# One fused two-layer kernel: the same instructions in other orders on all engines

## The chip, the cores and the metric

The kernel runs on one core of a Trainium2 chip. The metric is the device time of one execution in microseconds (us). Three runs of the kernel before took 1318.04, 1318.08 and 1318.75 us; the median is 1318.08.

## What is computed

Two layers over 64 sequences of 128 tokens with 256 features, each with a context of the same shape. Cut to what matters:

```python
# layer 0: attention with 16 heads of 16 features, over ctx
q, k, v = relu(x @ Wq + bq), relu(ctx @ Wk + bk), relu(ctx @ Wv + bv)
scores  = where(mask_of_query_row, q_ @ k_.T / 4, 1e-9)
x       = layernorm(softmax(scores) @ v_ + x) * gamma + beta
# layer 1, part 1: a Mamba-2 block
zxbcdt  = rms(x) @ in_proj_w                    # 256 -> 1288 features
z, xBC, dt = split(zxbcdt)
xBC     = silu(conv4(xBC))                      # causal, 4 taps, 768 features
h_t     = h_{t-1} * exp(dt*A) + (dt*xh_t) B_t ;  y_t = h_t C_t + D*xh_t   # 8 heads of 64
h       = x + rms(y * silu(z)) @ out_proj_w
# layer 1, part 2: attention with 8 heads of 32 features, over ctx
x       = h + softmax(ln(h) @ Wq @ (ctx @ Wk).T / sqrt(32)) @ (ctx @ Wv) @ Wo
```

## The kernel before

The 64 sequences are worked in 32 groups (g = 0 to 31) of two (b = 0, 1). Each engine has a program of its own: a list of small functions called in an order written out by hand, with waits on semaphores inside them. The body of `for g in range(NG - 9)` is the steady loop, 23 passes; the written-out lists before and behind it fill and empty the pipeline. In one pass an engine works on several groups at once: g+7 for the first projections, down to g+2 for the last part of the second attention.

TensorE's pieces (line of the matmul). Full array, 128 rows by 128 columns: `q`, `k`, `cp`, `z`, `k1` (six products each, twelve for z, L332: every weight and input is split in a high and a low part, three products for one), `v` (L375, L380), `v1` (L627), `o` (L573, and L575 for the sum of squares), `q1` (L587), `wp` (L692), `gm` (L531), `dp` (L490), and the transposes `tn` (L412), `ot`, `nt`, `bx`, `ht`, `tC` (L442) and `bd` (L501). Part of the array at a time: `sA` (L399) are the first attention's scores for the maxima, `sT` (L432, L436) the same scores transposed, `sC` (L648, L652) the second attention's scores. They use four groups of 32 rows. `av` (L456) and `oC` (L677) are the value products of the two attentions, on four groups of 32 columns, `y` (L556) the product of the Mamba block, on two groups of 64 columns. A matmul of plain float32 appears as two instructions in the trace, so one `av` is 8, one `sA` 16 and one `y` 16 instructions. `unread` repeats a product whose result nobody reads, in the lists before and behind the loop.

All results go to eight PSUM banks. The table `USES` fixes which piece uses which bank after which other one, and `bank(name, i, g)` gives the semaphore value at which the piece before in the same bank has been read. `sA(g, b)` takes four banks and waits for all four before its first matmul. For b = 0 one of them is bank 0, where `sT` number 7 of the group before stands; `eA(g, 7)` on ScalarE reads it (L1463). `y(g, b)` waits for `lg` on VectorE (L1024) and `xd` on GpSimd, `lg` for `gm` and `scan`; `yd` (L1044) reads y, and `v1` takes y's bank after it.

On the other engines: VectorE reads scores for maxima (`mA`, `mC`), does the convolution's taps (`tap`), the scan over time (`scan`), softplus (`dc`) and norms. ScalarE has exps (`eA`, `eC`), tanh (`th`, `zt`), copies out of PSUM and the high parts of the splits. GpSimd has the low parts (`lo_x`, `lo_c`, `lo_u`, `yl`), products by gates (`ga`, `xd`, `dx`) and powers. SyncE issues the transfers.

Of the kernel before, what the change touches and what calls it, by code (L numbers as in the profile page):

```python
# [12 lines left out]
NG = 32  # L13
# [24 lines left out]
def program(nc, a):  # L38
    with ExitStack() as ctx:
# [179 lines left out]
        def sync(e):  # L219
# [82 lines left out]
            load_x(1); load_c(1); load_t(0); load_m(1); load_x(2); load_m(2); load_c(2); load_c(3)  # L302
            load_m(3); load_x(3); load_t(1); load_x(4); load_m(4); dec_out(0); dec_in(0, 0); load_t(2); dec_in(0, 1)
            load_u(0); dec_out(1); load_c(4); dec_in(1, 0); dec_in(1, 1); load_u(1); load_t(3); load_x(5)
            dec_out(2); load_c(5); dec_in(2, 0); load_x(6); dec_in(2, 1); load_m(5); load_u(2); load_t(4)
# [10 lines left out]
            store(NG - 9); dec_out(NG - 6); load_c(NG - 3); dec_in(NG - 6, 0); load_m(NG - 3); load_m(NG - 2)  # L316
            dec_in(NG - 6, 1); load_x(NG - 2); load_u(NG - 6); load_t(NG - 4); load_c(NG - 2); store(NG - 8)
            dec_out(NG - 5); load_x(NG - 1); dec_in(NG - 5, 0); load_m(NG - 1); dec_in(NG - 5, 1); load_u(NG - 5)
            dec_out(NG - 4); load_c(NG - 1); load_t(NG - 3); dec_in(NG - 4, 0); dec_in(NG - 4, 1); load_u(NG - 4)
            load_u(NG - 3); load_t(NG - 2); store(NG - 7); dec_out(NG - 3); dec_in(NG - 3, 0); dec_in(NG - 3, 1)  # L320
            dec_out(NG - 2); store(NG - 6); load_t(NG - 1); load_u(NG - 2); dec_in(NG - 2, 0); dec_in(NG - 2, 1)
            store(NG - 5); dec_out(NG - 1); load_u(NG - 1); dec_in(NG - 1, 0); dec_in(NG - 1, 1); store(NG - 4)
# [4 lines left out]
        def tensor(e):  # L327
# [385 lines left out]
            k1(0, 1); bx(1, 0); av(2, 4); av(2, 5); av(2, 6); av(2, 7); sA(3, 0); ht(0, 0); ot(2, 1); q(4, 0)
            q(4, 1); ht(0, 1); k(4, 0); gm(1, 0); q1(0, 0); sA(3, 1); y(1, 0); v(4, 0); q1(0, 1); nt(2, 0); bx(1, 1)
            sC(0, 0); gm(1, 1); dp(2, 0); cp(2, 0); y(1, 1); cp(2, 1); o(1, 0); v1(0, 0); cp(2, 2); z(2, 0)
            tn(3, 0); cp(2, 3); o(1, 1); sT(3, 0); cp(2, 4); bd(2, 0); cp(2, 5); tn(3, 1); av(3, 0); av(3, 1)
            av(3, 2); av(3, 3); tC(0, 0); k(4, 1); ot(3, 0); z(2, 1); sT(3, 1); tC(0, 1); k1(1, 0); bx(2, 0)
            av(3, 4); av(3, 5); av(3, 6); av(3, 7); sA(4, 0); ot(3, 1); k1(1, 1); ht(1, 0); ht(1, 1); q(5, 0)
            tC(0, 2); q(5, 1); gm(2, 0); k(5, 0); sA(4, 1); y(2, 0); v(5, 0); q1(1, 0); q1(1, 1); gm(2, 1); bx(2, 1)
            nt(3, 0); tC(0, 3); sC(1, 0); oC(0, 0); oC(0, 1); dp(3, 0); cp(3, 0); cp(3, 1); y(2, 1); o(2, 0)  # L720
            v1(1, 0); z(3, 0); cp(3, 2); wp(0, 0); tn(4, 0); o(2, 1); cp(3, 3); sT(4, 0); bd(3, 0); cp(3, 4)
            cp(3, 5); tn(4, 1); av(4, 0); av(4, 1); av(4, 2); av(4, 3); tC(1, 0); k(5, 1); ot(4, 0); z(3, 1)
            sT(4, 1); tC(1, 1); k1(2, 0); bx(3, 0); av(4, 4); av(4, 5); av(4, 6); av(4, 7); sA(5, 0); k1(2, 1)
            ot(4, 1); ht(2, 0); ht(2, 1); q(6, 0); q(6, 1); tC(1, 2); k(6, 0); gm(3, 0); q1(2, 0); sA(5, 1); y(3, 0)
# [100 lines left out]
        def vector(e):  # L825
# [1291 lines left out]
```

## Time and profile before

| | |
|---|---|
| median of three runs | 1318.08 us |
| span of the profiled execution | 1319.5 us |
| TensorE matmuls busy | 1303.4 us (99%) |
| VectorE busy | 1193.6 us (90%) |
| ScalarE busy | 1131.2 us (86%) |
| GpSimd busy | 947.7 us (72%) |
| granted TensorE clock | 1.00 |

The span runs from the first to the last instruction. It is 1.4 us over the median of the runs. Busy is the time in which an engine had at least one instruction under way. Matmuls overlap: the next starts before the one before has left the array, so what a matmul costs is the time from its start to the start of the next, and not the duration beside it.

### The profile page before, as it was taken

The numbers are of one execution on the slowest core, as the hardware profiler recorded it, in microseconds if no ns is written. First come the engines' busy times: TensorE is split into PE (matmuls) and PEld (weight loads), VectorE is DVE, ScalarE is ACT, GpSimd is POOL, SyncE is SP. The second block draws the span as 40 slices with busy tenths as digits, with TensorE's granted clock in tenths as the row PEclk, the third lists the DMA queues.
The fourth block names the chain that finished last, engine by engine and source line by source line (L and its number), as shares of the span: only waits on it lengthen the run. The fifth ranks groups of instructions, "written<-read, shape, count | busy, mean of one in ns | idle before, by whom it ended". The sixth has DMA issues, their size and how long they took to land.

```text
span 1319.5 us, 43916 instructions
## 1 busy us (share of the span) xinstructions
PE 1303.4 (99%) x15877; PEld 1165.5 (88%) x15877; DVE 1193.6 (90%) x3032; ACT 1131.2 (86%) x3407; POOL 947.7 (72%) x1214
## 2 busy tenths in 40 slices
PE   8999999999999999999999999999999999999998
PEld 7888888999888898888998888899888889898887
DVE  6999999999999999999999999999999999999882
ACT  6778888898888898888898888899888899888866
POOL 4777777777777777777677777687777677677674
PEclk9999999999999999999999999999999999999999
DMA  6121122212122212122211122211122222011210
GB/s 208 48 74 50 50 74 78 78 49 67 50 70 78 78 50 66 50 70 78 78 57 59 50 70 78 78 60 57 50 70 78 77 82 62 17 51 58 66 49 25
DMA packets 41285, 87.03 MB, mean 66 GB/s; under 512 B 5744, under 2 KB 10992, under 8 KB 41072
## 3 DMA queue, kind: packets, MB, share of 16 engines
q1 hardware_dynamic: 40560, 83.93, 20.4%
q8 instruction: 129, 2.11, 0.7%
q14 instruction: 84, 0.69, 0.2%
q10 hardware_dynamic: 512, 0.31, 0.1%
HBM read 75.53 MB, written 8.68 MB: 64 GB/s over the span
## 4 chain that ended last, share of the span: by engine, by line
PE 92%; DVE 4%; POOL 2%; issue 1%; DMA 1%; ACT 1%; DVEq 0%; ACTq 0%; POOLq 0%
PE bank L332 28%; PE bank L442 11%; PE bank L573 7%; PE bank L432 5%; PE bank L399 5%; PE bank L456 5%; PE bank L556 5%; PE bank L587 4%; PE bank L692 4%; PE bank L627 3%; PE bank L380 3%; PE bank L648 3%; PE bank L677 2%; PE bank L490 2%; PE bank L436 1%; PE bank L531 1%
## 5 line engine op out<-in xcount | busy, mean ns | idle before, releaser
L991 DVE SCALAR_TENSOR_TENSOR ACC<-bank,cw,ACC 128x250 f32<-128x250 f32 (+2 forms) x576 | 264.5, 462 | 6.4 <-ACT ACC L1561 3.7
L332 PE MATMUL bank<-xnT,wnl 128*128 128x256 f32 x640 | 198.6, 310 | 1.7 <-DVE XC L1004 1.4
L1648 ACT ACTIVATE PC<-bank,stc 128x128 f32<-128x128 f32 x512 | 182.8, 388 | 8.0 <-DVE stc L1103 5.2
L332 PE MATMUL bank<-xnL,wnh 128*128 128x256 f32 x640 | 178.7, 279 | 0.0
L332 PE MATMUL bank<-xnT,wnh 128*128 128x256 f32 x640 | 178.3, 279 | 0.0
L835 DVE TENSOR_REDUCE sta<-bank 128x4 f32<-128x512 f32 x256 | 163.6, 672 | 2.8 <-PE bank L399 2.8
L1015 DVE TENSOR_TENSOR_SCAN L<-DB,id 128x1024 f32<-128x1024 f32 x64 | 146.6, 2290 | 2.2 <-DMA DB<-dec_scratch 2.2
L1967 POOL TENSOR_TENSOR PC<-PC,stc 128x512 f32<-128x512 f32 x128 | 132.4, 1043 | 11.7 <-DVE stc L1110 11.5
L1463 ACT ACTIVATE PTA<-bank 128x512 f32<-128x512 f32 x256 | 133.5, 629 | 6.8 <-PE bank L436 3.9
L332 PEld LDWEIGHTS bank<-xnT,wnl 128*128 128x128 f32 x640 | 120.4, 188 | 21.4 <-issue 16.2
L1922 POOL TENSOR_TENSOR XH<-XH,dtt 128x512 f32<-128x512 f32 x64 | 81.0, 1265 | 56.6 <-ACT XH L1578 56.6
L332 PEld LDWEIGHTS bank<-xnL,wnh 128*128 128x128 f32 x640 | 120.8, 189 | 0.1
L332 PEld LDWEIGHTS bank<-xnT,wnh 128*128 128x128 f32 x640 | 120.1, 188 | 0.0
L1648 ACT ACTIVATION_READ_ACCUMULATOR PC<-bank,stc 128x1 f32 x512 | 116.7, 228 | 0.0
L1847 POOL TENSOR_TENSOR cL<-cT,cH 128x512 fp32r<-128x512 f32 x31 | 59.0, 1903 | 76.8 <-ACT cH L1395 76.8
L1561 ACT ACTIVATE ACC<-bank,cw 128x256 f32<-128x256 f32 x192 | 110.6, 577 | 2.2 <-PE bank L332 1.5
L1931 POOL TENSOR_TENSOR Y<-Y,SZ 128x512 f32<-128x512 f32 x64 | 85.9, 1342 | 18.8 <-DVE Y L1044 16.1
L1937 POOL TENSOR_TENSOR Yl<-Y,Yh 128x512 fp32r<-128x512 f32 x64 | 82.2, 1285 | 17.4 <-ACT Yh L1606 17.4
L1449 ACT ACTIVATE NT<-bank,sel 128x128 fp32r<-128x128 f32 x256 | 73.6, 382 | 21.5 <-PE bank L412 21.5
L1662 ACT ACTIVATE PTC<-bank 128x512 f32<-128x512 f32 x128 | 78.8, 622 | 15.3 <-PE bank L442 15.2
L1103 DVE TENSOR_REDUCE stc<-bank 128x4 f32<-128x512 f32 x128 | 84.3, 681 | 6.9 <-PE bank L652 6.7
L1569 ACT ACTIVATE bank<-ACC 128x256 f32<-128x256 f32 x192 | 79.6, 418 | 11.1 <-DVE ACC L991 10.8
(210 smaller groups left out, 4757.7 us busy)
## 6 DMA issues: line engine op xcount, KB each, us to landing
DB<-dec_scratch SPq DMA_DIRECT2D x64, 512.0 KB, 4.0
cT<-in_cT SPq DMA_DIRECT2D x64, 256.0 KB, 2.7
xt<-in_xt SPq DMA_DIRECT2D x32, 256.0 KB, 3.7
out_x<-X SPq DMA_DIRECT2D x32, 256.0 KB, 4.0
xT<-in_xT SPq DMA_DIRECT2D x31, 256.0 KB, 4.1
QM<-qm_rows SPq DMA_DIRECT2D x31, 128.0 KB, 4.0
XC<-in_win SPq DMA_DIRECT2D x2, 644.0 KB, 6.8
PTC<-in_wout SPq DMA_DIRECT2D x2, 256.0 KB, 4.6
```

Source lines behind the costliest of these rows:

```text
L332: mm = e.matmul(t[:, c0:c0 + T], wt[:, k, m:m + 128], x[:, k, :], start=(n == 0), stop=(n == 5))
L442: mm = e.transpose(t[:, c0 + i * 128:c0 + (i + 1) * 128], src(i), ident[:, :])
L573: e.matmul(t[:, 0:256], x[:, kk * 128:(kk + 1) * 128], w[:, kk, :], start=(n == 0), stop=(n == 11))
L835: e.tensor_reduce(sta[ns % 4][:, 4 * j:4 * j + 4], t[:, :].rearrange("p (i k) -> p i k", i=4), AX_X, ALU.max, negate=True).then_inc(s_mA, 1)
L991: e.scalar_tensor_tensor(out=w, in0=t[:, 0:T].rearrange("p (b t) -> p b t", b=NB)[:, :, 0:125 + k], scalar=cw[:, c, k:k + 1], in1=w, op0=A ...
L1015: e.tensor_tensor_scan(L[:, :, :].rearrange("p h t -> p (h t)"), DB[b][:, :], id8[:, :, :].rearrange("p h t -> p (h t)"), 0.0, ALU.mult, A ...
L1103: e.tensor_reduce(stc[g % 4][:, 4 * i:4 * i + 4], t[:, :].rearrange("p (i k) -> p i k", i=4), AX_X, ALU.max, negate=True).then_inc(s_mC, 1)
L1463: e.activation(PTA[n % 4][:, :, :], t[:, :].rearrange("p (i k) -> p i k", i=4), ACT.Exp).then_inc(s_eA, 1)
L1561: e.activation(ACC[n % 3][:, :, :], t[:, 0:T].rearrange("p (b t) -> p b t", b=NB), ACT.Identity, bias=cw[:, c, 4:5], scale=cw[:, c, 3:4]). ...
L1648: op = e.activation(PC[n % 4][:, p, :], t[:, p * 128:(p + 1) * 128], ACT.Exp, bias=stc[g % 4][:, 4 * i + p:4 * i + p + 1], accum_out=stc[g ...
L1931: e.tensor_tensor(cv(Y[:, :]), cv(Y[:, :]), SZ[:, :, b * 128:(b + 1) * 128], ALU.mult).then_inc(s_ga, 1)
L1967: e.tensor_tensor(PC[n % 4][:, :, :], PC[n % 4][:, :, :], stc[g % 4][:, 16 + 4 * i:20 + 4 * i].unsqueeze(2).to_broadcast([128, 4, 128]), A ...
```

## The change

No function changes. The calls stand in another order in all five programs, in the loop and in the lists before and behind it; their number and kind are the same. TensorE's loop, cut to the part that differs (the first and last calls of the body are as before):

```diff
                 bx(g + 4, 0)
                 av(g + 5, 4)
                 av(g + 5, 5)
+                sA(g + 6, 0)
                 av(g + 5, 6)
                 av(g + 5, 7)
-                sA(g + 6, 0)
                 ht(g + 3, 0)
                 k1(g + 3, 1)
                 ot(g + 5, 1)
                 q(g + 7, 0)
                 ht(g + 3, 1)
                 q(g + 7, 1)
+                tC(g + 2, 2)
                 k(g + 7, 0)
-                tC(g + 2, 2)
                 gm(g + 4, 0)
                 q1(g + 3, 0)
                 sA(g + 6, 1)
+                v(g + 7, 0)
                 y(g + 4, 0)
-                v(g + 7, 0)
+                q1(g + 3, 1)
                 bx(g + 4, 1)
-                q1(g + 3, 1)
+                nt(g + 5, 0)
                 tC(g + 2, 3)
-                nt(g + 5, 0)
+                oC(g + 2, 0)
+                sC(g + 3, 0)
+                oC(g + 2, 1)
                 gm(g + 4, 1)
-                sC(g + 3, 0)
-                oC(g + 2, 0)
-                oC(g + 2, 1)
                 cp(g + 5, 0)
                 dp(g + 5, 0)
                 y(g + 4, 1)
                 cp(g + 5, 1)
                 o(g + 4, 0)
+                v1(g + 3, 0)
                 z(g + 5, 0)
-                v1(g + 3, 0)
+                wp(g + 2, 0)
                 cp(g + 5, 2)
-                wp(g + 2, 0)
                 tn(g + 6, 0)
```

Of the other engines' loops, the moves that the text below speaks of:

```diff
 # VectorE
+                mA(g + 7, 4)
                 x2(g + 6, 1)
-                mA(g + 7, 4)
-                yd(g + 5, 0)
                 mA(g + 7, 5)
                 mA(g + 7, 6)
                 mA(g + 7, 7)
+                yd(g + 5, 0)
                 scan(g + 5, 1)
...
                 mC(g + 4, 1)
-                mC(g + 4, 2)
                 d0(g + 6, 0)
                 d0(g + 6, 1)
+                nm(g + 7, 1)
+                mC(g + 4, 2)
                 rC(g + 4, 0)
                 tap(g + 6, 0)
-                nm(g + 7, 1)
 # ScalarE
                 hx(g + 2, 0)
+                split_c(g + 6)
                 pC(g + 1, 1)
-                split_c(g + 6)
...
+                v1e(g + 2, 0)
+                zt(g + 4, 0)
                 th(g + 4, 1)
-                zt(g + 4, 0)
-                v1e(g + 2, 0)
 # GpSimd
-                nC(g + 2, 1)
                 lo_u(g + 3)
                 qm(g + 6, 0)
                 r2(g + 3, 1)
+                lo_x(g + 7)
+                hr(g + 3, 0)
                 qm(g + 6, 1)
-                hr(g + 3, 0)
-                lo_x(g + 7)
+                nC(g + 2, 1)
                 hr(g + 3, 1)
 # SyncE
                 load_c(g + 6)
+                store(g)
+                load_m(g + 6)
                 dec_out(g + 3)
                 dec_in(g + 3, 0)
-                load_m(g + 6)
                 load_x(g + 7)
+                load_t(g + 5)
                 load_u(g + 3)
                 dec_in(g + 3, 1)
-                load_t(g + 5)
-                store(g)
```

The lists before and behind the loop are rearranged in the same manner, the places of `unread` and of the warming matmuls among them.

## Rows read from the trace of the kernel before

**Rows 1.** The page's busy times: us (share of the span) xinstructions.
```profile
PE 1303.4 (99%) x15877; PEld 1165.5 (88%) x15877; DVE 1193.6 (90%) x3032; ACT 1131.2 (86%) x3407; POOL 947.7 (72%) x1214
```

**Rows 2.** Busy time of the engines in three stretches: ahead of the loop, loop, behind.
```profile
0.00:206.00 206.00, 199.31 (x2384) 177.46 (x2385) 182.60 (x457) 166.37 (x467) 144.79 (x195) 1.00 0.26 82
206.00:1114.00 908.00, 907.92 (x11220) 814.27 (x11218) 845.45 (x2161) 803.25 (x2438) 665.22 (x851) 1.00 0.21 66
1114.00:1319.00 205.00, 196.21 (x2284) 173.72 (x2275) 165.58 (x415) 161.60 (x505) 137.68 (x170) 1.00 0.16 50
```

**Rows 3.** Waits, whole span: total us, times, longest.
```profile
PEld bank L456 <- ACT PTA L1463: 6.6, 33, 0.3
```

**Rows 4.** Timeline of TensorE, one pass: start us, us; av x4, sA, ht.
```profile
606.68 1.21 PE L456 MATMUL bank<-PTA,V 128*32 128x128 f32 x32
607.82 1.15 PE L399 MATMUL bank<-KT,QT 32*128 32x256 f32 x16
608.90 0.44 PE L442 MATMUL bank<-ident,xh 128*128 128x128 f32 x2
```

**Rows 5.** The same pass: q1, sA, y, v.
```profile
613.33 1.03 PE L587 MATMUL bank<-HT,wq 128*128 128x256 f32 x4
614.29 1.15 PE L399 MATMUL bank<-KT,QT 32*128 32x256 f32 x16
615.36 1.09 PE L556 MATMUL bank<-L,XH 128*64 128x128 f32 x16
616.39 0.50 PE L375 MATMUL bank<-vbias,onesr 128*128 128x512 f32 x1
```

**Rows 6.** The same pass: q1, tC, gm, sC, oC x2, cp, y.
```profile
618.53 1.03 PE L587 MATMUL bank<-HT,wq 128*128 128x256 f32 x4
619.40 0.60 PE L442 MATMUL bank<-ident,PC 128*128 128x128 f32 x4
...
620.27 0.39 PE L531 MATMUL bank<-XC 128*128 128x128 f32 x2
620.59 1.17 PE L648 MATMUL bank<-K1T,Q1T 32*128 32x128 f32 x32
...
621.91 1.08 PE L677 MATMUL bank<-PTC,V 128*32 128x128 f32 x32
622.92 0.38 PE L332 MATMUL bank<-xnT,wnl 128*128 128x256 f32 x1
623.14 0.28 PE L332 MATMUL bank<-xnL,wnh 128*128 128x256 f32 x1
623.26 0.28 PE L332 MATMUL bank<-xnT,wnh 128*128 128x256 f32 x1
...
624.61 1.09 PE L556 MATMUL bank<-L,XH 128*64 128x128 f32 x16
```

**Rows 7.** The other av run: whole, its second half, its last, tn.
```profile
638.87 1.08 PE L456 MATMUL bank<-PTA,V 128*32 128x128 f32 x32
...
639.33 0.62 PE L456 MATMUL bank<-PTA,V 128*32 128x128 f32 x16
...
639.55 0.40 PE L456 MATMUL bank<-PTA,V 128*32 128x128 f32 x8
...
639.88 0.33 PE L412 MATMUL bank<-ident,NM 128*128 128x128 f32 x1
```

**Rows 8.** Weight loads of the first av run's end [idle before <-releaser].
```profile
607.46 0.16 PEld L456 LDWEIGHTS bank<-PTA,V 128*32 128x32 f32 x8 [0.19 <-ACT PTA L1463]
```

**Rows 9.** Timeline of ScalarE: the four exps for this run.
```profile
605.28 2.13 ACT L1463 ACTIVATE PTA<-bank 128x512 f32<-128x512 f32 x4
```

**Rows 10.** Timeline of VectorE: lg(1) and yd(1).
```profile
622.70 1.21 DVE L1024 TENSOR_TENSOR L<-L,bank 128x1024 f32<-128x1024 f32 x1
...
626.41 0.69 DVE L1044 TENSOR_TENSOR Y<-bank,DX 128x512 f32<-128x512 f32 x1
```

**Rows 11.** Line 399: duration ns min/median/max, first and last start.
```profile
L399 PE MATMUL bank<-KT,QT x1024: 374/374/479, 14.2 to 1206.3; 32*128 32x256 f32 x171
```

More of the change, by code:

```diff
@@ L319, in sync @@
[L319 to L322, printed above, removed]
+            dec_out(NG - 6); load_c(NG - 3); dec_in(NG - 6, 0); store(NG - 9); load_u(NG - 6); load_x(NG - 2)
@@ new lines, in sync @@
+            dec_in(NG - 6, 1); load_m(NG - 3); store(NG - 8); load_x(NG - 1); dec_out(NG - 5); load_c(NG - 2)
+            load_t(NG - 4); load_m(NG - 2); dec_in(NG - 5, 0); load_t(NG - 3); load_u(NG - 5); dec_in(NG - 5, 1)
+            load_m(NG - 1); dec_out(NG - 4); load_c(NG - 1); dec_in(NG - 4, 0); store(NG - 7); load_u(NG - 4)
+            dec_in(NG - 4, 1); dec_out(NG - 3); load_t(NG - 2); dec_in(NG - 3, 0); store(NG - 6); load_t(NG - 1)
+            dec_in(NG - 3, 1); load_u(NG - 3); dec_out(NG - 2); dec_in(NG - 2, 0); load_u(NG - 2); dec_in(NG - 2, 1)
@@ L323, in sync @@
+            dec_out(NG - 1); store(NG - 5); dec_in(NG - 1, 0); dec_in(NG - 1, 1); store(NG - 4); load_u(NG - 1)
             store(NG - 3); store(NG - 2); store(NG - 1)
@@ new lines, in scalar @@
+            de(0, 1); de(0, 2); ac(0, 1); nt_(1, 0); dq(0, 0); th(0, 0); ac(0, 2); th(0, 1); qe(2, 1); zt(0, 0)
+            dd(0, 0); ac(0, 3); da(0, 0); ac(0, 4); th(0, 2); eA(1, 0); eA(1, 1); eA(1, 2); eA(1, 3); th(0, 3)
+            ac(0, 5); oa(1, 0); th(0, 4); nt_(1, 1); split_c(3); th(0, 5); ke(2, 1); zt(0, 1); eA(1, 4); eA(1, 5)
+            eA(1, 6); eA(1, 7); xhe(0, 0); oa(1, 1); n1(1, 0); qe(3, 0); qe(3, 1); n1(1, 1); nx(1, 0); xhe(0, 1)
+            nx(1, 1); ve(3, 0); nh(1, 0); nh(1, 1); qq(0, 0); yh(0, 0); de(1, 0); de(1, 1); de(1, 2); ac(1, 0)
@@ new lines, in scalar @@
+            ke(3, 0); dq(1, 0); ac(1, 1); th(1, 0); yh(0, 1); qq(0, 1); th(1, 1); zt(1, 0); ac(1, 2); nt_(2, 0)
+            split_x(4); dd(1, 0); ac(1, 3); th(1, 2); split_u(0); da(1, 0); eA(2, 0); eA(2, 1); ac(1, 4); eA(2, 2)
+            eA(2, 3); th(1, 3); ac(1, 5); oa(2, 0); nt_(2, 1); split_c(4); th(1, 4); th(1, 5); zt(1, 1); ke(3, 1)
+            eA(2, 4); eA(2, 5); eA(2, 6); eA(2, 7); hx(0, 0); hx(0, 1); n1(2, 0); oa(2, 1); xhe(1, 0); he(0, 0)
+            qe(4, 0); qe(4, 1); he(0, 1); ke(4, 0); q1e(0, 0); n1(2, 1); xhe(1, 1); nx(2, 0); ve(4, 0); nx(2, 1)
@@ new lines, in scalar @@
+            q1e(0, 1); nh(2, 0); nh(2, 1); yh(1, 0); split_x(5); qq(1, 0); eC(0, 0); ac(2, 0); de(2, 0); de(2, 1)
+            de(2, 2); eC(0, 1); dq(2, 0); ac(2, 1); eC(0, 2); th(2, 0); yh(1, 1); qq(1, 1); th(2, 1); split_u(1)
+            zt(2, 0); v1e(0, 0); dd(2, 0); ac(2, 2); nt_(3, 0); eC(0, 3); da(2, 0); th(2, 2); ac(2, 3); eA(3, 0)
+            eA(3, 1); eA(3, 2); eA(3, 3); ac(2, 4); th(2, 3); oa(3, 0); ke(4, 1); ac(2, 5); pC(0, 0); nt_(3, 1)
+            th(2, 4); th(2, 5); hx(1, 0); zt(2, 1); eA(3, 4); eA(3, 5); eA(3, 6); eA(3, 7); split_c(5); he(1, 0)
@@ new lines, in scalar @@
+            oa(3, 1); pC(0, 1); xhe(2, 0); hx(1, 1); qe(5, 0); qe(5, 1); he(1, 1); pC(0, 2); q1e(1, 0); n1(3, 0)
+            n1(3, 1); ke(5, 0); nx(3, 0); ve(5, 0); nx(3, 1); q1e(1, 1); pC(0, 3); nh(3, 0); nh(3, 1); xhe(2, 1)
+            qq(2, 0); yh(2, 0); eC(1, 0); oT(0, 0); ac(3, 0); ac(3, 1); de(3, 0); de(3, 1); eC(1, 1); de(3, 2)
+            eC(1, 2); qq(2, 1); dq(3, 0); zt(3, 0); th(3, 0); yh(2, 1); ac(3, 2); th(3, 1); v1e(1, 0); split_u(2)
+            eC(1, 3); dd(3, 0); nt_(4, 0); ac(3, 3); da(3, 0); th(3, 2); eA(4, 0); eA(4, 1); eA(4, 2); eA(4, 3)
@@ new lines, in scalar @@
+            split_c(NG - 3); xhe(NG - 6, 0); oa(NG - 5, 1); hx(NG - 7, 1); n1(NG - 5, 0); he(NG - 7, 0); qe(NG - 3, 0)
+            qe(NG - 3, 1); he(NG - 7, 1); pC(NG - 8, 2); q1e(NG - 7, 0); nx(NG - 5, 0); ke(NG - 3, 0); n1(NG - 5, 1)
+            nx(NG - 5, 1); ve(NG - 3, 0); xhe(NG - 6, 1); q1e(NG - 7, 1); nh(NG - 5, 0); pC(NG - 8, 3); nh(NG - 5, 1)
+            yh(NG - 6, 0); qq(NG - 6, 0); oT(NG - 8, 0); eC(NG - 7, 0); split_x(NG - 2); ac(NG - 5, 0); de(NG - 5, 0)
+            eC(NG - 7, 1); de(NG - 5, 1); ac(NG - 5, 1); de(NG - 5, 2); eC(NG - 7, 2); yh(NG - 6, 1); v1e(NG - 7, 0)
@@ new lines, in scalar @@
+            split_u(NG - 5); v1e(NG - 6, 0); zt(NG - 4, 0); split_x(NG - 1); dd(NG - 4, 0); ac(NG - 4, 2)
+            nt_(NG - 3, 0); eC(NG - 6, 3); da(NG - 4, 0); ac(NG - 4, 3); th(NG - 4, 2); eA(NG - 3, 0); eA(NG - 3, 1)
+            eA(NG - 3, 2); eA(NG - 3, 3); ac(NG - 4, 4); ac(NG - 4, 5); th(NG - 4, 3); oa(NG - 3, 0); nt_(NG - 3, 1)
+            pC(NG - 6, 0); th(NG - 4, 4); ke(NG - 2, 1); zt(NG - 4, 1); split_c(NG - 1); th(NG - 4, 5); eA(NG - 3, 4)
+            eA(NG - 3, 5); eA(NG - 3, 6); eA(NG - 3, 7); hx(NG - 5, 0); pC(NG - 6, 1); xhe(NG - 4, 0); oa(NG - 3, 1)
@@ L1829, in gpsimd @@
+            eC(NG - 1, 3); pC(NG - 1, 0); v1e(NG - 1, 0); pC(NG - 1, 1); pC(NG - 1, 2); pC(NG - 1, 3); oT(NG - 1, 0)
         def gpsimd(e):
```

626 lines of the change are left out of this document (292 added, 334 removed).

## The prediction

> **What bounds the kernel now.** I read the busy times of the page first: TensorE is busy for 1303.4 of 1319.5 us [rows 1]. The table of stretches then says where the rest is [rows 2]: 6.7 us idle in the first 206 us, 8.8 in the last 205, and 0.1 in the 908 us between, which are the 23 passes of the steady loop (39.5 us each). The granted clock is 1.00 in all three, the upper level of 2.4 GHz. In the loop VectorE has 845 and ScalarE 803 us of work for TensorE's 908. So one pass lasts as long as TensorE's matmuls take one after the other, and a change of order matters by what it does to the time from one matmul's start to the next. The waits that TensorE does pay in the loop are small: the one with the longest total at the weight loads of the value products is 6.6 us in 33 places [rows 3]; a run of four av that has it takes 1.14 us (606.68 to 607.82) where one without takes 1.01 [rows 4, 7].
>
> **How a piece's time depends on its neighbour.** I read starts in TensorE's timeline and subtract. Two kinds of pieces exist. Full-array ones (q, k, v, cp, z, all transposes, gm, q1) use 128 rows and columns. Part-array ones use four groups of 32 rows (sA, sT, sC), four of 32 columns (av, oC) or two of 64 columns (y).
>
> - A full-array piece pays when a part-array one follows. Four q1 matmuls take 0.87 us before a transpose (618.53 to 619.40) and 0.96 before sA (613.33 to 614.29) [rows 5, 6]. Price of that edge: 0.09.
> - A full-array piece pays when it follows a part-array one: the first product after oC holds the array 0.22 us (622.92 to 623.14), the next one 0.12 (to 623.26) [rows 6]. Price 0.10.
> - A part-array run pays at both of its ends whatever stands there. Four av between full-array pieces: the first two 0.46, the third 0.22, the last 0.33, together 1.01 [rows 7]. So the last costs 0.11 over the middle one and the first 0.02. Two oC take 1.01 as well, though they stand behind sC and not behind a full-array piece [rows 6]. sA takes 1.07 before y and 1.08 before a transpose, and the sA behind av is no shorter than the one behind q1 [rows 4, 5]. y takes 1.03 behind sA and in front of v [rows 5].
>
> The last point is what this change turns on: a part-array piece beside an unlike part-array piece pays as much as beside a full-array one. The Trainium skill says the same, in TensorEngine Tiling (Array Packing), Key Properties: "Changing tiling mode (not just tile) drains the TensorE". By that sentence the count of changes of shape is the thing to sum, and the trace agrees, at 0.13 to 0.2 us for a pair of edges.
>
> **The change part by part.** Nothing is added or removed. In TensorE's loop I count the places where the array's shape changes: 17 in a pass before, 20 after.
>
> 1. sA(g+6,0) goes between the second and third of four av. One run of av becomes two: a second last (+0.11) and a second first (+0.02). sA itself stays at 1.08. +0.13.
> 2. sC goes between the two oC, with the same sum for oC: +0.13. gm moves behind the last oC and takes over the entry that cp paid; tC takes over the exit that gm paid. Nothing for those.
> 3. v goes between sA(g+6,1) and y, which stood together, and q1 follows y. v's entry behind sA is the one it had behind y. New are v's exit (0.09) and the entry of q1 (0.10, that of the product behind oC; q1's are twice as long, so bounds 0 and 0.2): +0.19.
> 4. Full-array pieces changed among themselves (tC before k, nt before tC, v1 before z, wp before cp): no change of shape, so 0 for each. A first product behind another kind of full-array piece could cost up to the 0.10 of an edge; bounds -0.1 and +0.1 a pass.
>
> Sum 0.45 us a pass, 0.15 per change of shape. Over 23 passes 10.4. The written-out orders before and behind the loop have 31 changes of shape more than before (157 before, 188 after, counted from the diff): at 0.15 each 4.7. Together 15.1 us.
>
> 5. A wait moves. sA(g+6,0) takes four banks at once, one of them the bank of sT piece 7, which the eighth exp, eA(g+5,7), frees. In the pass shown the four exps end at 605.28 + 2.13 = 607.41 and the load for the waiting av follows at 607.46 [rows 8, 9]. After the change sA is next in line at 607.25 (the av run starts at 606.68 [rows 4], and two av take 0.24 + 0.33). It would start at about 607.46, 0.21 late, and behind it wait av 6 and 7. The 0.13 that av 7 loses there today goes, because it is then 1.3 us later. Net +0.08, which I round to 0.1 a pass, 2.8 us for the 28 groups that have this order or nearly this. Bounds: 0, if ScalarE reaches its exps earlier, and 0.3.
>
> 6. VectorE: mostly small exchanges; its instructions keep their durations, and it is not the bound in the loop [rows 2]. One chain gets tight. y(g+4,1) needs lg(1) (1.21 us), which needs gm(g+4,1). Today lg starts at 622.70 and ends at 623.91, and y starts at 624.61: 0.70 to spare [rows 6, 10]. After, gm is just ahead of cp and dp, so from its start to y there are 0.22 + 1.69 = 1.91 us, out of which 0.49 go for gm, some 0.1 for the signal and 1.21 for lg: 0.1 to spare. I take 0, bounds 0 and 0.3 a pass. The yd behind it (626.41) then comes some 0.7 later, and v1, which needs its bank and is itself earlier, has 0.3 left by the same subtraction.
>
> 7. ScalarE, GpSimd and the queue of transfers: split_c before pC, v1e before zt, nC(1) behind hr, store ahead of load_m. Each piece moved has over 0.5 us until TensorE needs it; two are nearer, xhe(1) before oC(0) and xhe(0) before q, at 0 to 0.1. At nothing, with bounds of 0 and 0.1 a pass each. Stores wait for fin of a much earlier group and hold back only loads for groups two to three passes ahead.
>
> Sum: 15.1 + 2.8 = 17.9 us on the profiled 1319.5, which is 1337.4. The profile's span is 1.4 over the median of the three runs (1318.08), so the time should be **1336 us**.
>
> **Rivals.**
>
> *New waits add up* (items 6 and 7). In favour: the chain gm, lg, y has 0.1 left of 0.7, and a late lg pushes yd, ga and o. Against: each is under 0.1 by my sums, and each pass is now longer, which gives every other engine 0.6 us more. At 0.3 a pass over 28 passes 8.4: 1345 us.
>
> *The ends gain.* TensorE idles 15.5 us outside the loop [rows 2], and every engine's order there is new. If half of it goes, 7.8 us: 1329 us. For: the pool is there. Against: most of those waits are of filling and emptying the pipeline, which no order shortens.
>
> *Unlike pieces hide each other*, the other side. If a piece sandwiched between unlike part-array pieces (sA between av, sC between oC) had neither edge to pay, because its groups load while the others still run, then four edges would go: 0.11 out of the column-shaped piece, 0.10 into the row-shaped one (sA's matmuls last 374 ns at the median and 479 at most, which I take for the first of a run [rows 11]), 0.11 out of it taken like av's, 0.02 into the next; 0.34 a sandwich, 0.68 a pass. With the 0.45 that come, -0.23 a pass, -6.4 over 28: 1312 us. It decides from 0.45 saved a pass on. The Trainium skill has a rule this way: TensorE: Matmul & The Clock Gate, Part 3, has weight loads overlap running matmuls when the row groups differ. The same edges stand in the trace at full price, so this needs the new neighbours to behave as the old ones don't.
>
> *The order hardly matters*: TensorE's loop stays at 39.5 because the extra edges fall into time lost anyway. Against: there is 0.1 us of idle in 908. 1318 us.
>
> **How the numbers follow.** Forecast 1336 with 0.57 (own range 1331 to 1340), new waits 0.22, the ends 0.12, hiding 0.05, no matter 0.04. 0.2% is 2.6 us, about what a measurement of this kernel can tell from none. Slower 0.91, same 0.04, faster 0.05. The range reaches from the case of the ends less the error of the 31 edges there (1327) to the waits with a little on top (1348).
>
> **What would show it.** Right: passes of 40.0 to 40.2 us instead of 39.5; each run of two av at 0.57 and each oC at 0.57; v before y over 0.09 longer than today; a wait of sA on the exps of about 0.2 in most passes. Wrong: sA between av shorter than 1.07; a pass below 39.8; a wait in front of y or v1 of over 0.1; idle outside the loop that changes by more than 5 us.

## The result and the profile after

The changed kernel takes 1394.82 us (median of 4 runs, 1393.70 to 1398.23) against 1318.17 for the kernel before on the same chip: ratio 1.058, 95% interval 1.0564 to 1.0596. It is slower, as forecast, but by 76.6 us and not by 18, and 47 us outside the range.

The page's busy times, to hold against [rows 1]:

```profile
PE 1332.0 (96%) x15877; PEld 1167.2 (84%) x15877; DVE 1269.7 (91%) x3032; ACT 1130.8 (81%) x3407; POOL 1023.3 (74%) x1214
```

The three stretches, cut where the loop starts and ends now (the loop's first k has moved from 205.8 to 225.0 us, the first piece behind the loop from 1114.7 to 1177.1):

```profile
0.00:225.00 225.00, 206.22 (x2383) 178.74 (x2384) 191.94 (x460) 166.98 (x467) 148.83 (x195) 0.99 0.23 78
225.00:1177.00 952.00, 926.69 (x11226) 815.60 (x11225) 903.87 (x2159) 803.17 (x2439) 728.53 (x850) 1.00 0.19 62
1177.00:1391.00 214.00, 199.09 (x2273) 172.86 (x2271) 173.94 (x415) 160.69 (x503) 145.94 (x170) 1.00 0.15 50
```

What the reader is to see: the same instructions, and in the loop the clock as before [rows 2] (ahead of it 0.99 for 1.00: one stretch of 3.4 us at the lower level of 1.2 GHz, from 17.3 us on), but TensorE has 25 us idle in the loop where it had 0.1, and VectorE and GpSimd are *busy* for 58 and 63 us longer in it without an instruction more. Of TensorE's 18.8 us of extra busy time in the loop 10.8 are the changes of shape, counted below; the rest isn't broken down. The idle 25 are new. A pass lasts 41.4 us (952.1 / 23) where it lasted 39.5. So the loop is 43.2 us longer, the lists ahead of it 19.2 and those behind it 9.9.

The waits of the whole span (total us, times, longest), to hold against [rows 3]:

```profile
PEld bank L573 <- issue: 19.5, 27, 1.0
PEld bank L399 <- DVE K1T L1092: 15.9, 23, 0.8
```

Before, L573 waited 0.8 us in 4 places and L399 never for K1T. L573 is `o`, the output projection; L399 is `sA`, which now waits for a bank that VectorE's kk1 (K1T) frees. By TensorE's starts they cost 0.8 and 0.5 us in a pass (medians). With the 0.47 of the edges, below, that is all of the 1.8 us by which a pass is longer.

### Where the pass waits

TensorE's timeline of the pass that answers to [rows 4] (start us, us):

```profile
643.87 0.64 PE L456 MATMUL bank<-PTA,V 128*32 128x128 f32 x16
644.96 1.15 PE L399 MATMUL bank<-KT,QT 32*128 32x256 f32 x16 [0.45 <-DVE K1T L1092]
646.04 0.64 PE L456 MATMUL bank<-PTA,V 128*32 128x128 f32 x16
646.61 0.44 PE L442 MATMUL bank<-ident,xh 128*128 128x128 f32 x2
```

and those that answer to [rows 5, 6] (the first product of v, y, q1, bx; oC, sC, oC, gm; then the first product of o):

```profile
653.09 0.50 PE L375 MATMUL bank<-vbias,onesr 128*128 128x512 f32 x1
...
654.90 1.09 PE L556 MATMUL bank<-L,XH 128*64 128x128 f32 x16
655.92 1.13 PE L587 MATMUL bank<-HT,wq 128*128 128x256 f32 x4
656.89 0.60 PE L442 MATMUL bank<-ident,XC 128*128 128x128 f32 x4
...
658.29 0.65 PE L677 MATMUL bank<-PTC,V 128*32 128x128 f32 x16
658.87 1.17 PE L648 MATMUL bank<-K1T,Q1T 32*128 32x128 f32 x32
659.86 0.40 PE L652 MATMUL bank<-maskb,onesb 3*128 3x512 bf16 x4
660.19 0.65 PE L677 MATMUL bank<-PTC,V 128*32 128x128 f32 x16
660.76 0.49 PE L531 MATMUL bank<-XC 128*128 128x128 f32 x2
...
665.33 0.36 PE L573 MATMUL bank<-woutl,Yh 128*128 128x256 f32 x1 [0.67 <-issue]
```

Subtract starts as in the prediction: two av 0.57 (646.04 to 646.61), sA 1.08, v 1.81 where it took 1.71 at the median, q1 0.97 behind y where it took 0.87, each oC 0.58 or 0.57. Those are the predicted edges. What is not in the prediction is the 0.45 ahead of sA and the 0.67 ahead of o (0.51 and 0.82 at the median of the loop's passes, by starts).

### Why they wait

VectorE in the same pass, first ahead of sA, then from y's evacuation (L1044) on:

```profile
643.26 1.31 DVE L897 SCALAR_TENSOR_TENSOR xa<-xa,sta,gam 128x256 f32<-128x256 f32 x1
644.49 0.41 DVE L1092 TENSOR_TENSOR K1T<-bank,keep 128x256 f32<-128x256 f32 x1
...
655.02 1.87 DVE L835 TENSOR_REDUCE sta<-bank 128x4 f32<-128x512 f32 x3
656.82 0.67 DVE L1044 TENSOR_TENSOR Y<-bank,DX 128x512 f32<-128x512 f32 x1
657.41 2.27 DVE L1015 TENSOR_TENSOR_SCAN L<-DB,id 128x1024 f32<-128x1024 f32 x1
```

GpSimd in the same two stretches:

```profile
643.25 1.04 POOL L1959 TENSOR_TENSOR PC<-PC,stc 128x512 f32<-128x512 f32 x1
...
657.63 3.12 POOL L1923 TENSOR_TENSOR Y<-Y,SZ 128x512 f32<-128x512 f32 x1 [0.97 <-DVE Y L1044]
660.72 1.04 POOL L1914 TENSOR_TENSOR XH<-XH,dtt 128x512 f32<-128x512 f32 x1
661.72 1.04 POOL L1905 TENSOR_TENSOR DX<-XC,pc 128x512 f32<-128x512 f32 x1
662.72 1.27 POOL L1929 TENSOR_TENSOR Yl<-Y,Yh 128x512 fp32r<-128x512 f32 x1
663.95 0.74 POOL L1935 TENSOR_TENSOR SQ<-SQ 128x256 f32<-128x256 f32 x1
664.77 0.46 POOL L1937 TENSOR_TENSOR SQ<-SQ 128x128 f32<-128x128 f32 x1
```

and the same places of the kernel before, first VectorE, then GpSimd:

```profile
616.60 0.69 DVE L1044 TENSOR_TENSOR Y<-bank,DX 128x512 f32<-128x512 f32 x1 [0.26 <-PE bank L556]
617.21 1.88 DVE L835 TENSOR_REDUCE sta<-bank 128x4 f32<-128x512 f32 x3
619.00 2.28 DVE L1015 TENSOR_TENSOR_SCAN L<-DB,id 128x1024 f32<-128x1024 f32 x1
```

```profile
617.44 1.29 POOL L1931 TENSOR_TENSOR Y<-Y,SZ 128x512 f32<-128x512 f32 x1
620.64 1.48 POOL L1922 TENSOR_TENSOR XH<-XH,dtt 128x512 f32<-128x512 f32 x1 [1.92 <-ACT XH L1578]
```

Read them side by side. Before, yd (L1044) came ahead of three maxima (L835), whose input is in PSUM, and GpSimd's ga (L1931; L1923 in the changed file) ran beside those in 1.29 us. After, yd stands behind the maxima and just ahead of the scan, which reads two operands from SBUF, and the same ga takes 3.12 us: it ends at 660.75, 1.07 after the scan. What then stands ahead of o is a queue, not a slow instruction: XH, DX, Yl, SQ, until 665.23, and o loads its weights at 665.29. The 1.31 us of L897 (0.48 before) are the same thing the other way: it starts with GpSimd's PC at 643.25, which ends at 644.29, and ends 0.28 after it; kk1 and sA are late by it.

The Trainium skill has this rule, in SBUF — State Buffer, SBUF: two separate sides: the port pair that VectorE and GpSimd share is "an **exclusive lock**, not a bandwidth split", held for a whole instruction, and a VectorE operation with two SBUF inputs shuts out a GpSimd one that reads SBUF. The trace agrees, in both directions (3.12 for 1.29, 1.31 for 0.48), but for about 0.2 us in which the two still overlap.

### The profile page after: what moved, and what is told of

Its sections match the earlier page's. It is cut to its first block, busy times and chain, and to the rows that moved or that the text cites. A ratio compares the mean times of both kernels' runs of the same rounds, so it can differ in the third digit from the quotient of the medians.

```text
span 1391.9 us, 43916 instructions
## 1 busy us (share of the span) xinstructions
PE 1332.0 (96%) x15877; PEld 1167.2 (84%) x15877; DVE 1269.7 (91%) x3032; ACT 1130.8 (81%) x3407; POOL 1023.3 (74%) x1214
## 4 chain that ended last, share of the span: by engine, by line
PE 47%; DVE 24%; ACT 15%; issue 7%; POOL 4%; DMA 1%; SPq 0%; DVEq 0%; ACTq 0%; POOLq 0%
PE bank L332 13%; PE bank L442 5%; DVE ACC L991 5%; ACT PC L1644 5%; PE bank L399 5%; PE bank L587 3%; PE bank L573 3%; PE bank L556 3%; ACT PTA L1459 3%; PE bank L692 3%; DVE XC L1004 2%; DVE xa L897 2%; DVE sta L835 2%; PE bank L627 2%; ACT ACC L1557 2%
## 5 line engine op out<-in xcount | busy, mean ns | idle before, releaser
L835 DVE TENSOR_REDUCE sta<-bank 128x4 f32<-128x512 f32 x256 | 163.8, 670 | 11.8 <-PE bank L399 11.7
L1015 DVE TENSOR_TENSOR_SCAN L<-DB,id 128x1024 f32<-128x1024 f32 x64 | 153.4, 2398 | 1.2 <-DMA DB<-dec_scratch 1.0
L1923 POOL TENSOR_TENSOR Y<-Y,SZ 128x512 f32<-128x512 f32 x64 | 128.3, 2005 | 33.8 <-DVE Y L1044 33.0
L1959 POOL TENSOR_TENSOR PC<-PC,stc 128x512 f32<-128x512 f32 x128 | 135.6, 1060 | 17.0 <-DVE stc L1110 16.9
L1557 ACT ACTIVATE ACC<-bank,cw 128x256 f32<-128x256 f32 x192 | 114.0, 595 | 17.0 <-PE bank L332 17.0
L1644 ACT ACTIVATION_READ_ACCUMULATOR PC<-bank,stc 128x1 f32 x512 | 122.0, 238 | 0.0
L1839 POOL TENSOR_TENSOR cL<-cT,cH 128x512 fp32r<-128x512 f32 x31 | 83.6, 2698 | 33.0 <-ACT cH L1391 33.0
L573 PE MATMUL bank<-woutl,Yh 128*128 128x256 f32 x256 | 75.2, 294 | 15.1 <-issue 14.2
L1024 DVE TENSOR_TENSOR L<-L,bank 128x1024 f32<-128x1024 f32 x64 | 77.9, 1218 | 11.2 <-PE bank L531 10.8
L399 PE MATMUL bank<-KT,QT 32*128 32x256 f32 x1024 | 73.6, 401 | 13.4 <-DVE K1T L1092 9.7
```

The source lines that it names most:

```text
L399: mm = e.matmul(ts[j][:, m * 256:(m + 1) * 256], QT[g % 2][r, m, b * 128:(b + 1) * 128], KT[g % 2][r, m, b, :, :], start=True, stop=True)
L573: e.matmul(t[:, 0:256], x[:, kk * 128:(kk + 1) * 128], w[:, kk, :], start=(n == 0), stop=(n == 11))
L835: e.tensor_reduce(sta[ns % 4][:, 4 * j:4 * j + 4], t[:, :].rearrange("p (i k) -> p i k", i=4), AX_X, ALU.max, negate=True).then_inc(s_mA, 1)
L1015: e.tensor_tensor_scan(L[:, :, :].rearrange("p h t -> p (h t)"), DB[b][:, :], id8[:, :, :].rearrange("p h t -> p (h t)"), 0.0, ALU.mult, A ...
L1557: e.activation(ACC[n % 3][:, :, :], t[:, 0:T].rearrange("p (b t) -> p b t", b=NB), ACT.Identity, bias=cw[:, c, 4:5], scale=cw[:, c, 3:4]). ...
L1644: op = e.activation(PC[n % 4][:, p, :], t[:, p * 128:(p + 1) * 128], ACT.Exp, bias=stc[g % 4][:, 4 * i + p:4 * i + p + 1], accum_out=stc[g ...
```

## The experiments

"Pass" is the sum of the median start-to-start times of TensorE's pieces over the loop's 23 passes (before 39.50 us, after 41.29). The lists ahead of the loop, the loop and the lists behind it were exchanged separately. Each ratio is to runs of the kernel before on the same chip, with its 95% interval.

**loop_only**: all five loops changed, everything around them as before. **te_loop**: TensorE's loop alone.

> The changed orders in the 23 loop passes of all five engines, the lists before and behind as in the kernel before. Theory A (waits inside the pass: y comes behind v, its sum yd and the gate ga come late, ga meets the scan, o waits; and sA waits for kk1): passes near the 41.3 us of the changed kernel, 1318 + 23 x 1.85 = about 1361. Rival B (the loss is made in the filling list and the loop only carries a phase on): passes near 40.0, about 1330.

> Only TensorE's loop in the changed order, every other engine as before. Theory A (TensorE's late y is the cause): at least 1.2 us a pass, 1345 to 1370, because VectorE's yd now stands and waits for y. Rival C (the new orders on the other engines are the cause, TensorE's order costs only its changes of shape, 0.45 a pass, and the sA wait): 1328 to 1332.

Measured: loop_only 1367.3, ratio 1.0359 [1.0343, 1.0374], pass 41.28; both waits are there as in the changed kernel (av to sA 0.85, cp to o 1.63). te_loop 1392.81, ratio 1.056 [1.0533, 1.0587], pass 42.41, above what either theory said: TensorE's order on the other engines' old lists costs more in the loop than all the changed loops together, chiefly by waits ahead of cp (1.2 us a pass) and sA (0.5). The profile names

```profile
PEld bank L332 <- DVE xnL L923: 23.3, 20, 1.4
PEld bank L399 <- DVE K1T L1092: 14.1, 20, 0.8
```

(waits of te_loop, 240 to 1100 us). For sA the name is wrong here: K1T ends at 639.93, and sA, behind the two av, starts at 640.48, 0.36 behind the eighth exp (638.00 + 2.12 = 640.12):

```profile
638.00 2.12 ACT L1463 ACTIVATE PTA<-bank 128x512 f32<-128x512 f32 x4
639.51 0.42 DVE L1092 TENSOR_TENSOR K1T<-bank,keep 128x256 f32<-128x256 f32 x1
640.48 1.15 PE L399 MATMUL bank<-KT,QT 32*128 32x256 f32 x16 [0.46 <-ACT PTA L1463]
```

The two distances are the same at the median of the loop (0.36 and 0.56), and in no trace with sA between av does it start less than 0.36 behind this exp; behind K1T it starts from 0.05 on. So a changed order must be read as one plan; the other engines' moves took back 1.1 us of a pass. Not all of te_loop's time is waits: in the profiled run the granted clock fell seven times to 0.50 (1.2 GHz) for 3.4 us, which can cost 12 us in all by an estimate (half of 7 x 3.4), so the pass by medians is the safer number.

**b_sC**: the kernel before with one of TensorE's moves; **b_vyq**: with two.

```diff
 b_sC                        b_vyq
-                sC(g + 3, 0)                -                y(g + 4, 0)
                 oC(g + 2, 0)                                 v(g + 7, 0)
+                sC(g + 3, 0)                +                y(g + 4, 0)
                 oC(g + 2, 1)                +                q1(g + 3, 1)
                                                              bx(g + 4, 1)
                                             -                q1(g + 3, 1)
```

> The kernel before with one exchange in TensorE's loop: sC between the two oC. Two changes of shape more: 0.13 us a pass, 3.0 us, 1321. Both theories A and D say this, unless the later sC makes mC and lg late, then up to 1325. If unlike part-array pieces hid each other it would be 1318 or less.

> The kernel before with one exchange in TensorE's loop: v(g+7,0) ahead of y(g+4,0), and q1(g+3,1) ahead of bx(g+4,1). Two changes of shape more a pass, 0.19 us, 4.4 us in all. Theory A: y is 1.8 us later, VectorE waits for it in front of yd, ga and the scan follow late, o waits: 0.8 to 1.8 us a pass on top, 1340 to 1365. Rival D (only changes of shape count): 1322 to 1323.

Measured: b_sC 1323.2, ratio 1.0024 [1.0014, 1.0034], pass 39.65: +0.14, one pair of edges and nothing else. (By the prediction's count each of the two kernels has one change of shape more in a pass, 18 for 17; the two that the expectations name are the two edges of it.) b_vyq 1357.06, ratio 1.0278 [1.0258, 1.0298], pass 41.05: the edges are 0.2 of the 1.55. The rest is waits, the largest at cp: 1.63 us from oC to cp where it is 0.55. Its releaser (waits of b_vyq, 240 to 1100 us):

```profile
PEld bank L332 <- DVE xnL L923: 26.5, 21, 1.5
```

y comes 1.8 us later behind v, so yd, scan and nl come later on VectorE, and cp needs nl. In the prediction I had priced this move by its edges alone (0.19).

**l_yv**, **l_yv_yd**, **l_nC**: from loop_only, moves taken back. **b_scan**: from before, only the scan moved, so that ga meets it.

```diff
 l_yv (TensorE)              l_yv_yd (l_yv, and VectorE)
-                v(g + 7, 0)                 +                yd(g + 5, 0)
                 y(g + 4, 0)                                  mA(g + 7, 5)
+                v(g + 7, 0)                                  ...
                                             -                yd(g + 5, 0)
 l_nC (GpSimd)               b_scan (VectorE)
-                xr(g + 5, 0)                                 yd(g + 5, 0)
                 nC(g + 2, 2)                +                scan(g + 5, 1)
-                rs(g + 5, 0)                                 mA(g + 7, 5)
                 nC(g + 2, 3)                                 ...
+                xr(g + 5, 0)                -                scan(g + 5, 1)
+                rs(g + 5, 0)
```

> The kernel with all five changed loops (passes of 41.28 us), and in TensorE's loop v(g+7,0) back behind y(g+4,0). TensorE gets y 1.8 us earlier and loses no change of shape (sA, y, v, q1, ...: two fewer, -0.19 us a pass). Theory A: the late y is the first cause, but VectorE's yd still stands behind mA 5 to 7 and is followed at once by the scan, so the gate ga still runs into the scan; o's wait (0.82 us) goes only in part: 1345 to 1360. Rival F (only y's place on TensorE counts): 1335 to 1340.

> As l_yv, and VectorE's yd(g+5,0) back ahead of mA(g+7,5). Theory A: ga then runs beside the reductions and ends before the scan; o's wait goes. Left are the changes of shape (0.26 a pass) and sA's wait for kk1 (0.53): passes near 40.4, 1340 to 1346. Rival F: as l_yv, within 2 us.

> The kernel with all five changed loops, and in GpSimd's loop nC(g+2,2) and nC(g+2,3) back ahead of xr(g+5,0). Theory G: nC on GpSimd stretches VectorE's xs from 0.48 to 1.31 us (and x2), because both read two SBUF operands; kk1 behind it is late and sA(g+6,0), which needs kk1's bank, waits 0.53 us. Then xs is near 0.5 again, sA's wait falls to 0.1 to 0.2: 1355 to 1360. Rival H: sA waits for the eighth exp, as predicted, and the stretch of xs is no matter: 1365 to 1369, wait unchanged.

> The kernel before with one move on VectorE: scan(g+5,1) right behind yd(g+5,0), ahead of mA 5 to 7. It puts GpSimd's ga(g+4,0) beside the scan, which it isn't in the kernel before. Theory I (a GpSimd operation and a VectorE one with two SBUF inputs exclude each other): ga takes 3.0 to 3.6 us instead of 1.29 in every pass. Rival J (ga was long in the changed kernel for another reason): 1.3 us. The time: o(g+4,0) had over 1.6 us to spare, so up to 3 us more than before, 1318 to 1325.

Measured: l_yv 1368.24, ratio 1.0369 [1.0347, 1.0391], pass 41.29: nothing gained, outside both forecasts. Its 0.2 of edges are saved, but o still waits 0.72, and nt and tC wait 0.29 more. l_yv_yd 1350.86, ratio 1.0232 [1.0214, 1.0251], pass 40.58: o's wait is gone (0.82 with it). l_nC 1365.39, ratio 1.0347 [1.0329, 1.0364], pass 41.21: the mean of L897 falls from 890 to 481 ns and sA's wait from 0.51 to 0.10, but bx now waits 0.29 for VectorE's last XC, because the freed item pushed xr and with it bs. The 0.10 that is left is not shown to be the eighth exp's: sA still starts when K1T is done (628.56), as at the median of the loop, where it is 0.05 behind K1T and 0.49 behind the exp:

```profile
628.14 0.42 DVE L1092 TENSOR_TENSOR K1T<-bank,keep 128x256 f32<-128x256 f32 x1
628.62 1.15 PE L399 MATMUL bank<-KT,QT 32*128 32x256 f32 x16
```

b_scan 1340.5, ratio 1.0157 [1.0142, 1.0172]: a single move on VectorE makes 21 us, where at most 7 were expected. The mean of ga and of the lo_c split in the loop (240 to 1100 us), in b_scan and then in l_yv_yd:

```profile
L1931 POOL TENSOR_TENSOR Y<-Y,SZ 128x512 f32<-128x512 f32 x42 | 92.1, 2193 | 24.7 <-DVE Y L1044 22.2
L1847 POOL TENSOR_TENSOR cL<-cT,cH 128x512 fp32r<-128x512 f32 x21 | 40.2, 1914 | 57.9 <-ACT cH L1395 57.9
```

```profile
L1847 POOL TENSOR_TENSOR cL<-cT,cH 128x512 fp32r<-128x512 f32 x21 | 65.6, 3123 | 24.6 <-ACT cH L1395 24.6
L1931 POOL TENSOR_TENSOR Y<-Y,SZ 128x512 f32<-128x512 f32 x42 | 53.7, 1278 | 9.3 <-DVE Y L1044 9.3
```

ga's mean is 2193 ns where it meets the scan in one of its two places, 1278 where it doesn't, and 1286 before. That is the lock, made and unmade by one move. In b_scan ga starts at 626.07 beside a scan of 625.84 to 628.12 and takes

```profile
626.07 3.12 POOL L1931 TENSOR_TENSOR Y<-Y,SZ 128x512 f32<-128x512 f32 x1
```

the 3.12 of the changed kernel to the digit. Of b_scan's 0.9 us a pass most is not ga, though: tC(3) waits for its bank, which the maximum mA(5) frees, and that now stands behind the scan (0.73 us a pass).

```profile
628.75 0.66 PE L442 MATMUL bank<-ident,PC 128*128 128x128 f32 x4 [0.56 <-DVE sta L835]
```

And o doesn't wait in b_scan, where ga is long but yd is early; nor in b_vyq, where yd waits for a y that is 1.8 us later but ga has its 1.28 us (the mean in the loop). It waits where both come together, in the changed kernel, loop_only and l_yv. So the lock alone isn't o's price, and neither is the late yd.

**l_fix**: l_yv_yd and l_nC together. **l_gp**: l_yv_yd with GpSimd's whole loop as before.

> The kernel with all five changed loops and the three repairs together: v behind y on TensorE, yd ahead of mA 5 to 7 on VectorE, nC(2) and nC(3) ahead of xr on GpSimd. Theory A with G: o's wait and most of sA's wait are gone; left are 18 changes of shape instead of 17 a pass as counted (0.26 us), 0.1 for the exps and small waits of 0.1 to 0.3: passes of 39.9 to 40.2, 1328 to 1336. Rival K (the loop has another bottleneck that moves in, as kk1's wait did in the run with nC alone): 40.4 or more, over 1340.

> The changed loops of all engines but GpSimd, whose loop is the one before; v stands behind y on TensorE and yd ahead of mA 5 on VectorE as before. Lists ahead of and behind the loop as before. Theory P (GpSimd's moved items are what is left: k1 to bx 0.27 us for the late last xc, bx to nt and nt to tC 0.25 us, the late kk1 0.4 us): the pass falls from 40.58 us to the shape changes of the two scores between products (0.28) and the wait for the eighth exp (0.1) over 39.51, so 39.9 us, and the time to 1329 us (1325 to 1333). Rival C (the remaining waits belong to ScalarE's and VectorE's orders): the pass stays at 40.3 us or more, the time at 1337 us or more.

Measured: l_fix 1348.87, ratio 1.0222 [1.0207, 1.0237], pass 40.50; l_gp 1355.4, ratio 1.028 [1.0263, 1.0297], pass 40.89. Neither reached the hoped 39.9 to 40.2; in both the rival came true, that other waits move in. In l_fix the pass is 1.0 over before: 0.28 for the two sandwiches (sA between av, sC between oC; 19 changes of shape, not the 18 of the expectation), 0.10 ahead of sA, which again starts 0.05 behind K1T, 0.27 at bx, 0.25 at nt and tC behind it, 0.08 at bd. So the named moves were the largest, and behind each the next wait stood within 0.1 to 0.3 us. l_gp shows that GpSimd's old order isn't the remedy either: it suited VectorE's old list, and here GpSimd waits 35 us for the reciprocals that the changed VectorE list brings later:

```profile
L1967 POOL TENSOR_TENSOR PC<-PC,stc 128x512 f32<-128x512 f32 x84 | 86.4, 1036 | 35.3 <-DVE stc L1110 35.3
```

**front_only**, **f_vector**, **fx_gpsimd**: only the lists ahead of the loop changed; on all engines, on VectorE alone, on all but GpSimd.

> Only the lists ahead of the loop in the changed order, on all engines; loops and the lists behind as before. Theory L (the filling lists cost time of their own, 19 us in the changed kernel before the first pass): 1335 to 1339. Rival M (most of those 19 us is a phase that the old loop wins back): 1322 to 1328.

> Only VectorE's list ahead of the loop in the changed order, everything else as before. If VectorE's order there (it waits 6.8 us for sA against 2.8 before) is the cause of the 19 us: 1330 or more. If it is TensorE's list, as in the loop: 1320 to 1324.

> The changed lists ahead of the loop on all engines but GpSimd, which keeps its old one. If the lock between GpSimd and VectorE makes the loss in front, by where GpSimd's operations fall: at least 5 us under the run with all five. If TensorE, ScalarE and VectorE make it among themselves: within 3 us of it.

Measured: 1340.92, 1340.66 and 1342.95; ratios 1.0161 [1.0146, 1.0176], 1.0166 [1.0149, 1.0183], 1.0178 [1.0163, 1.0194]. VectorE's list alone makes a loss as large as all lists together. TensorE's moves there (12 of the extra changes of shape stand ahead of the loop, 84 before and 96 after, 1.8 us by the forecast) add nothing to it that intervals of 2 us can show; TensorE's list wasn't changed alone. Nor does GpSimd's list matter for it (fx_gpsimd).

**v_whi, v_s1, v_s2, v_s3**: VectorE's front list in four stretches between which nothing moves, each changed by itself.

```diff
-            w_hi(0)
-            mA(0, 0); mA(0, 1); mA(0, 2); mA(0, 3); nm(0, 0); nw(0, 0); mA(0, 4); mA(0, 5); mA(0, 6); mA(0, 7)
+            mA(0, 0); mA(0, 1); mA(0, 2); mA(0, 3); nm(0, 0); nw(0, 0); mA(0, 4); mA(0, 5); w_hi(0); mA(0, 6); mA(0, 7)
```

> The kernel before with one move ahead of the loop: VectorE's w_hi(0), the high part of the layer's weights, stands behind mA(0,5) and not at the very start. Theory M (many small delays): 0 to 1 us, 1318 to 1320. Rival W (this move makes the first layer weights late, and everything behind them): 3 us or more, 1321 or more, up to the whole 20 us.

> The kernel before with VectorE's list changed only from mA(0,6) up to lg(0,1), the first 65 us or so. In the run with the whole changed list TensorE is 4 us late at that point. Theory M: 2 to 5 us, 1320 to 1323. Rival W: under 1 us, since the weights' move is not in it.

> The kernel before with VectorE's list changed only from d0(1,0) up to yd(2,0), some 65 to 150 us. In the run with the whole changed list the lateness grows from 4 to 10 us over it. Theory M (delays add up because TensorE has next to no idle time to lose them in): 5 to 8 us, 1323 to 1326. Rival E (echo: most of it is handed down from the first stretch and vanishes with it): under 2 us.

> The kernel before with VectorE's list changed only behind scan(2,1), some 150 to 206 us. In the run with the whole changed list the lateness grows from 10 to 20 us over it, with the longest single step, 2.95 us, at bx(3,0). Theory M: 7 to 11 us, 1325 to 1329; the four stretches together give 18 to 22 us. Rival E: under 3 us.

Measured, with ratios to a before of 1319.02: 1318.59 (0.9999 [0.9989, 1.0009]), 1322.62 (1.0025 [1.0014, 1.0037]), 1327.59 (1.0062 [1.0044, 1.0079]), 1328.11 (1.0067 [1.0047, 1.0087]). The sum of the excesses is 0.0153, 20 us, against f_vector's 0.0166. No single move did it; it is many small delays that add up. That the lists before and after differ there by moves of 10 to 23 places of items that TensorE needs late (nm, nw, rC, hm), ahead of conv taps that it needs soon, fits it; which of them costs what wasn't tried.

**loop_back**: front as before, loop and lists behind it changed.

> The lists ahead of the loop as before, the loop and the lists behind it changed. The changed loop alone gave 1367.3. Theory B (the lists behind the loop cost their own 10 us, as the changed kernel's last stretch shows): 1377 us (1374 to 1380). Rival H (the 10 us come with the late hand-over of front and loop): 1370 us or less.

Measured: 1374.97, ratio 1.0423 [1.0407, 1.0438]. The lists behind the loop cost 0.0064, 8 us, over loop_only. That bears out the 1377 of theory B. The account closes: front 0.0161, loop 0.0359, back 0.0064, together 0.0584 for a measured 0.058. Why the lists behind cost it wasn't looked into.

None of the variants beats the kernel before by more than the noise.

## Why the prediction was wrong, by its own steps

- **Bound of the kernel.** "A change of order matters by what it does to the time from one matmul's start to the next" was true of the kernel before. It made me price a change of order as TensorE's affair, and carry the other four engines' orders at 0 to 0.3 a pass.
- **Steps 1 to 4, the edges.** Right in mechanism and size, in the changed kernel as well as alone. 0.45 a pass forecast, 0.47 found, each term within 0.02 where nothing waits; b_sC has one of them alone, 0.14 for 0.13. The hiding rival is dead: sA between av takes 1.08. Over 23 passes that is 10.8 us of the loop's 43.2.
- **Step 5, the eighth exp.** The place was right, sA does wait; the bank and the size were not. In the changed kernel another of sA's banks comes last, K1T's, and the wait is 0.51. Of four banks I had looked at one. The exp comes last in te_loop, and costs 0.53 there: I let sA follow the exp after 0.05, as av does [rows 8, 9], and it takes 0.36. What the exp alone would cost in the changed kernel no run shows.
- **Step 6, VectorE. This is the step that failed.** "Its instructions keep their durations" is false. In the loop L897 went from 478 to 891 ns, L909 from 479 to 811, and on GpSimd ga from 1286 to 2117 and the lo_c split from 1937 to 3132, as new pairs met at the shared ports. "It is not the bound" was no reason: an engine below its full share still has items with a date. I checked the late y for the chain gm, lg, y (0.1 to spare; right, y(1) doesn't wait) and not for the chain of the other y, which the move of v pushes by 1.8 us and VectorE's list by three maxima more: yd, ga, XH, DX, Yl, SQ, o. It is the 0.8. VectorE's move is the one that counts: with v taken back o waits 0.72 (l_yv), with yd taken back too nothing (l_yv_yd).
- **Step 7, GpSimd.** "At nothing" failed as well. I named the move of nC(1) and not that of nC(2) and nC(3) behind xr(g+5,0), which is in the change too: nC stretches xs (L897) and delays kk1, 0.41 of sA's wait (l_nC). That is 9 us in the loop, though taking it back alone took 0.07 off the pass, since bx was next.
- **The 31 edges outside.** 4.7 us forecast, 29.1 found in the profile (19.2 ahead, 9.9 behind). The mechanism was the wrong one: VectorE's list ahead of the loop by itself costs 21 us (f_vector). The table of stretches had the hint [rows 2]: VectorE was busy for 182.6 of the first 206 us, so there was hardly room for anything late.
- **Rivals.** "New waits add up" was the right kind and was priced at 8.4 us where about 32 came in the loop, because I bounded each piece by the slack of the nearest rows and no piece by the resource that two engines share. The range rested on those bounds. "The ends gain" came out the other way, 29 us lost, and "hardly matters" is dead with a pass of 41.3. (By my own terms the new waits came to 1344 and the ends to 1328, not to 1345 and 1329.)

## What to carry to other kernels

Where a kernel's order is written out for all engines, price a move by following the moved result through every engine to the next TensorE piece that needs it, by starts and slack, and do the edges last. Before taking a duration over from the old trace, look who runs beside it on the other of VectorE and GpSimd: a span that stands with two lengths for one shape is the sign. And one move taken back tells what that wait costs only if the next in line has slack; take several back together before you trust the sum.

## What the runs showed of the hardware

The cost of meeting at the shared ports, in this kernel: a GpSimd product of 1.29 us took 3.12 beside a VectorE scan of 2.28, a VectorE operation of 0.48 took 1.31 beside a GpSimd one of 1.04. About 0.2 us of each runs beside the other's (ga ends 1.07 after the scan, not 1.29; L897 0.28 after PC, not 0.48). Reductions out of PSUM beside the same product left it at 1.29. It was in the kernel before too: XH takes 1.48 us where it meets the end of a scan (620.64, above) and 1.04 at 660.72 in the changed kernel. I had read such rows and not asked why.

The granted clock moved as well. The profile of the kernel before has it at 1.00 throughout; that of te_loop has seven stretches of 3.4 us at 0.50, of which this is the first (the third number from the right is TensorE's granted clock):

```profile
316.10:319.50 3.40, 3.40 (x22) 3.07 (x18) 3.37 (x11) 3.37 (x17) 1.59 (x3) 0.50 0.00 0
```

Shortly before, TensorE had been idle for 0.99 us ahead of cp (which starts at 313.81). In the stretch the products of cp and o start 0.21 us apart (317.23, 317.44), and at the upper level behind it 0.12 (319.56, 319.68). The timed runs of the changed kernel have a mean clock of 0.995 to 0.999, so by an estimate at most 6 us of its median are of this kind (at 0.996, 0.004 x 1395 / 0.5 = 11 us at half speed); the profiled run, with one such stretch, took 1393.7. What sets it off isn't shown: the profile of loop_back, with the same waits in its loop, has no such stretch in 1373 us.
